# In a three-stage transformer block, VectorE empties the PSUM bank of a batch's first spikes during the choice of experts

## What is computed

```
x = L0(x)                          # 8-head softmax attention over 1024 tokens, output projection, residual
t = tokens of x                    # (8, 1024, 128)

# L1, spiking attention on the normalised tokens
z  = layernorm(t)
sq = (z @ Wq.T >= 0.25);  sk = (z @ Wk.T >= 0.25);  sv = (z @ Wv.T >= 0.3)
router_mask = causal(sq @ sk.T) > 0.1
t = t + router_mask @ sv

# L2, one expert of 8 for each token, on the newly normalised tokens
z2    = layernorm(t)
prob  = softmax(z2 @ Wr + br);  route = argmax(prob);  p_max = max(prob)
t = t + (gelu(z2 @ W1[route] + b1[route]) @ W2[route] + b2[route]) * (p_max / p_max)
```

## Time and profile before

| what | value |
|---|---|
| time, median of 3 runs | 1195.29 us (1194.04 to 1195.98) |
| the profiled execution's own time | 1197.78 us |
| its span (first to last instruction) | 1196.0 us |
| TensorE matmul busy | 1090.4 us, 91% of the span |
| VectorE busy | 878.4 us, 73% |
| ScalarE busy | 779.3 us, 65% |
| GpSimd busy | 322.6 us, 27% |

### The profile page before, as it was taken

The page is one execution under the profiler, slowest core; times in us unless marked ns, Lnnn a source line. Parts: engine busy times, 40 slices in busy tenths (PEclk is TensorE's granted clock), DMA queues, the critical chain, the costliest instruction groups (busy, mean ns, idle before and its releaser), DMA issues. The chain is left out here.

```text
span 1196.0 us, 23744 instructions
## 1 busy us (share of the span) xinstructions
PE 1090.4 (91%) x8040; PEld 535.9 (45%) x8048; DVE 878.4 (73%) x2004; ACT 779.3 (65%) x1691; POOL 322.6 (27%) x379
## 2 busy tenths in 40 slices
PE   5999999999999999999999999998889852899994
PEld 2223333333333333333333333334567541899993
DVE  4889889888988987987988898851666753455545
ACT  2167777777877877787777787786665431455553
POOL 4131041031113104104103110052325555344450
PEclk7599999999999999999999999999998965899996
DMA  5519008206504702800830550000601011222229
GB/s 130 113 44 171 22 6 180 50 8 132 104 2 93 143 1 54 162 22 2 179 56 2 110 108 2 2 19 1 175 15 33 27 32 55 59 68 70 66 60 283
DMA packets 73244, 85.53 MB, mean 72 GB/s; under 512 B 15544, under 2 KB 57144, under 8 KB 71592
## 3 DMA queue, kind: packets, MB, share of 16 engines
q1 hardware_dynamic: 64712, 72.91, 28.2%
q0 software_dynamic: 4320, 8.89, 2.2%
q10 hardware_dynamic: 4096, 2.23, 0.8%
HBM read 57.08 MB, written 26.65 MB: 70 GB/s over the span
## 5 line engine op out<-in xcount | busy, mean ns | idle before, releaser
L733 DVE TENSOR_REDUCE neg_half<-slot 128x1 f32<-128x512 f32 x1024 | 633.9, 682 | 103.6 <-PE slot L508 85.6
L647 ACT ACTIVATE probs<-ring 128x512 f32<-128x512 f32 x1024 | 528.8, 602 | 137.1 <-PE ring L517 134.7
L517 PE MATMUL ring<-stack_q,stack_k 50*128 50x512 bf16 (+1 forms) x2048 | 420.8, 383 | 1.9
L559 PE MATMUL acc<-probs,v_sb 128*32 128x512 f32 x2048 | 274.0, 607 | 0.0
L517 PEld LDWEIGHTS ring<-stack_q,stack_k 50*128 50x128 bf16 (+1 forms) x2048 | 152.6, 93 | 258.0 <-issue 110.7
L510 PE MATMUL slot<-twin_k,twin_q 48*128 48x512 bf16 x512 | 183.2, 393 | 20.0 <-DMA twin_q<-parts_dram 11.9
L508 PE MATMUL slot<-stack_k,stack_q 48*128 48x512 bf16 x512 | 163.0, 394 | 2.8 <-DVE neg_half L733 2.8
L1566 ACT ACTIVATE zt<-bank,b_of 128x128 f32<-128x128 f32 x284 | 81.2, 369 | 86.9 <-PE bank L1534 63.4
L423 POOL CAST m_parts<-neg_max 128x16 bf16<-128x16 f32 x32 | 6.3, 198 | 381.3 <-DVE neg_max L739 381.3
L1509 POOL DMA_INDIRECT rows_tok<-zt,x_in x71 | 68.0, 958 | 89.5 <-DVE zt L1594 86.9
L510 PEld LDWEIGHTS slot<-twin_k,twin_q 48*128 48x128 bf16 x512 | 47.7, 94 | 94.5 <-DVE neg_half L733 72.7
(11 more groups left out here) (161 smaller groups left out, 1114.7 us busy)
## 6 DMA issues: line engine op xcount, KB each, us to landing
parts_dram<-parts SPq DMA_DIRECT2D x30, 384.0 KB, 5.7
stack_k<-parts_dram SPq DMA_DIRECT2D x16, 384.0 KB, 6.1
stack_q<-parts_dram SPq DMA_DIRECT2D x32, 192.0 KB, 7.4
x_in<-rows_in SPq DMA_DIRECT2D x71, 64.5 KB
xp<-in_x SPq DMA_DIRECT2D x8, 512.0 KB, 4.9
stack_k<-parts_dram SPq DMA_DIRECT2D x16, 256.0 KB, 3.7
xr<-in_x SPq DMA_DIRECT2D x8, 512.0 KB, 3.9
out<-zt SPq DMA_DIRECT2D x16, 256.0 KB, 2.1
```

Source lines behind the costliest of these rows:

```text
L517: return pe.matmul(out[:, :], stack_k[s % STACK_BUFS][rows, h, kt * P:(kt + 1) * P], stack_q[s % STACK_BUFS][rows, half, h, :], start=star ...
L559: mm = pe.matmul(acc[32 * h:32 * h + 32, :], v_sb[s // G % 2][:, kt, s % G * HG + h, :], probs[:, j % PROBS, h, :], start=(kt == 0), stop= ...
L647: act.activation(probs[:, j % PROBS, h, :], ring[n % S_BANKS][:, :], ACT.Exp).then_inc(s_empty[n % S_BANKS], 1)
L733: dve.tensor_reduce(neg_half[q % 2][:, half, k:k + 1], slot[n % M_BANKS][:, :], AX.X, ALU.max, negate=True).then_inc(m_empty[n % M_BANKS], 1)
```

## The change

VectorE's step for spike00 of batch r+1 moves forward. It stood behind `variances(r - 1)`, first of the round's spike steps; now it stands inside `choose`, behind the third operation (`beside(2)`) and its BN_STATS. This is done where `early(r)` holds, that is in rounds 2 to 6, five in all. No operation is added or taken away, and no other engine's program is changed.

```diff
@@ -1369,10 +1369,19 @@
+        def early(r):
+
+            return 2 <= r and r + 1 < B
+
         def choose_and_spread(r):
 
+            def beside(k):
+                spread(r - 1, k)
+                if k == 2 and early(r):
+                    spiked(("spike", r + 1, (0, 0)))
+
             if r >= 2:
-                choose(r - 2, lambda k: spread(r - 1, k))
+                choose(r - 2, beside)
             else:
                 for k in range(KT):
                     spread(r - 1, k)
@@ -1422,7 +1431,8 @@
         for job in STAGE:
             kind, b, args = job
             if kind == "spike":
-                spiked(job)
+                if args != (0, 0) or not early(b - 1):
+                    spiked(job)
```

## The result

The changed kernel takes 1202.64 us (median of 7 runs, 1200.19 to 1203.5), the kernel before beside it on the same chip 1194.04 us (7 runs). The ratio, which is taken over all runs of both kernels and not from the two medians, is 1.006 with a 95% interval of 1.0046 to 1.0075: slower by 7.2 us (5.5 to 9.0). The medians alone lie 8.6 us apart. The prediction had +3.3 us. Its direction holds, its size is less than half of what was measured, and the median lies 0.6 us above the end of its range, 1202.0 us.

What follows compares the result with a forecast made beforehand. Handovers set the pace, with a VectorE chain through var and GpSimd's root ending last; chain 2.3, late bank 0 and clock 1.0 gave 3.3 us on the 1195.3 us median: 1198.6 us, range 1194.6 to 1202.0.

Steps and rivals of the forecast that it cites:

- Steps (1) and (2): VectorE: the step put before L1362 delays var by 0.60 us; removing it behind var only adds idling, nothing comes back.
- Step (3): TensorE: spike10 need not wait; the 2.25 us break into smaller pauses further down, the last, before diag1, about 2 us.
- Step (4): Five rounds to count0: 5 x 0.60 less 0.7 us of slack, 2.3 us, passed on whole behind count0.
- a sign of being wrong: Behind count0: if the time there changes, the prediction is wrong; it had no term for this.
- Step (5): VectorE's moved step may wait for TensorE's spike00 at the low clock; bounds 0 and 0.6 us, taken as 0.
- Step (6): TensorE's spike_v0 and spike_v1: clock falls of 0.8 or 2.0 us; bounds 0 and 6 us, one round at 1.0 taken.
- A: TensorE's clock stays up, so only the chain slips: +2.3 us, 1197.6 us; chance 0.28.
- B: VectorE: the step is hidden in the choice's waits and rounds 2 to 4 lose their slack: 1194.6 us; chance 0.08.
- C: TensorE's pause before spike10 was the bound; 9.7 us won in all, near 1185.6 us; chance 0.03.
- D: Late spike00 bank, 0.6 us, and clock falls in two or three rounds: 1200.2 to 1204.2 us; chance 0.11.

Runs made afterwards that it cites:

- filled version: Changed kernel plus seven unused matrix products in TensorE's pause in front of diag1, in rounds 2 to 6; 1202.88 us, ratio 1.0047 to the kernel before.
- the swapped transposes: Kernel before with a round's transposes ordered turn2_0, turn0, turn2_1, turn1 instead of turn0, turn1, turn2_0, turn2_1; 1194.4 us, ratio 0.9983.
- the root's move: Kernel before with VectorE's statistics ahead of the choice, and GpSimd's inverse root at the round's start, before the scatters; 1189.33 us, ratio 0.9942.
- the new order: Kernel before with VectorE's statistics and variances ahead of most of the choice, TensorE's sums moved behind spike_v1; 1193.79 us, ratio 0.9974.

## Why the prediction was right, and where it was too small

The direction came out by the mechanism that was forecast: a second chain through `var` and GpSimd's root, which ends with the wait that the change removes. The size did not, and the median lies past the end of the range. Of the 5.81 us that the rounds grew, the chain is 2.06; the rest is falls of the clock and a late bank, for which 1.0 us stood in the sum, less 1.03 us of shorter tails, for which it had no term.

**Steps (1) and (2), the chain: right.** L1362 starts 0.59 us behind the moved step, `shift` stayed 1.96 us behind `var`, and nothing came back behind it; VectorE idled 1.16 to 1.20 us. The kernel with an unrelated operation in the same place gave the same 0.60 us.

**Step (3), TensorE: right.** spike10 waits no more, and the pause moved down to spike11 (1.08 us) and diag1 (1.81 us, where about 2 was said).

**Step (4), the sum of the chain: right for the heads, wrong behind them.** 2.3 us was said; it was 2.06 in the changed kernel and 2.3 where neither the clock nor the logits' wait disturbed it. The step added that everything behind count0 is passed on whole. It is not: a tail is 7.6 or 8.5 us and more, depending on the logits' wait for ScalarE. Before had one long tail, the changed kernel none (-1.03 us in sum), and a version in which the clock stays up has three (+1.9 us). The prediction named this as the thing for which it had no term, and as a sign of being wrong. The error helped it: the shorter tails brought the total 1.03 us nearer to the forecast.

**Step (5), the late bank: too small.** 0 was taken, between bounds of 0 and 0.6 us. It came to 1.07 us in two rounds, past both bounds, and to 1.3 to 1.6 us in the versions with filling. The reason given, that the round begins later against the clock's changes, held for round 6 and not for rounds 3 and 4, where the clock now fell at the start of the round (at about 889.6 and 910.1 us), as it had not before. The step sat where VectorE reaches it 0.5 us behind TensorE's end at the high clock, and at the low clock the product takes 0.8 to 0.9 us more.

**Step (6), the clock: too small, and the largest miss.** One round at 1.0 us was taken, and it was four rounds at 0.54 to 1.23, 3.71 us. The price of a fall was about right (0.8 to 2.0 us was said, and one came cheaper); their number was not. Since the falls of rounds 3 to 5 went with short tails, their net cost is less: the filled version without them is only 0.4 us shorter in its rounds. So the clock term and the tails have to be priced together.

**The rivals.** *A*, the clock stays up, at +2.3 us: the filled version is this case made by hand, and its rounds are 5.4 us longer. So A's premise would not have led to its time, on the trace of that version. *B* (hidden) and *C* (TensorE's pause the bound) fell with the heads. *D*, +4.9 to +8.9 us by the late bank and falls in two or three rounds, has the measured time in it and both of its mechanisms in the trace, though with four falls for two or three; it had a chance of 0.11.

The rule that the prediction weighed, from the Trainium skill, page "TensorE: Matmul & The Clock Gate", section "HAM oscillation — how this bites in real kernels", would have kept the clock up when the long pause was cut in pieces. The trace disagrees here: the longest pause went from 2.25 to 1.81 us and the granted clock over 870 to 965 us from 0.92 to 0.87, with falls in four rounds on work that VectorE gates. Filling the pause before diag1 did raise it, to 0.96 (with the swapped transposes from 0.91 to 0.93); filling the one before spike10 in the kernel before did not, 0.89.

## What to carry to other kernels

Before a step is pulled forward to end a visible wait, find the chain that ends together with it: here it ran through `var` and GpSimd's root, and the 0.60 us in front of `var` was paid in every round, less 0.2 to 0.3 us where TensorE had been the later one. The move that pays is the opposite one, to put what the chain needs (the statistics) first and what has slack (the choice) behind. Each such move must be followed into the next queue of the chain: without the root's move the new order was 3.1 us faster than before, with it 6.9 us, and a late root behind GpSimd's scatters was one visible part of the difference. When a term of the sum depends on the clock, price the work behind it too, because a wait there may take back what a faster clock gives: here 2.90 of 3.30 us.

## What was not expected of the hardware

- GpSimd's power over 128x8 float32 took 2.04 us instead of 1.67 while VectorE added two SBUF operands of 128x512 float32. Beside VectorE steps that read PSUM it stayed at 1.67. The Trainium skill, page "GPSIMD Engine Reference", section "1. Specifications", says that GpSimd's way to SBUF is contended by VectorE instructions with two SBUF inputs; the trace agrees, and the size here is 0.37 us.
- Nine more products in TensorE's longest pause lowered the mean granted clock from 0.92 to 0.89, while seven in another pause of the changed kernel raised it from 0.87 to 0.96. The first two are single executions, and over the whole program the runs of the kernel before and of the one with nine products can't be told apart (0.932 to 0.944 and 0.932 to 0.942); the rise with seven is in all runs. So the length of the longest pause alone does not tell what the clock will be.
- Open: in the reworked kernel without the root's move VectorE stood 2.41, 3.13 and 3.15 us ahead of L1352 at the end of rounds 3 to 5, which the trace puts down to no engine of the core (with the root's move once, 2.34 us; with the swap as well, in no round). The first of them:

```profile
913.35 0.23 DVE L1352 TENSOR_REDUCE col<-ps_logit 128x8 f32<-128x64 f32 x1 [2.41 <-remote]
```

- Open too: where the clock falls in a round differs between kernels whose order of instructions is nearly the same, and no run here settles what decides it.
